# Half of K projected earlier, SyncE's list reordered, and the rows of maxima split straight from PSUM

## The reference, cut to what matters

```python
x = x + xattn(layernorm(x), ctx)
# inside: 16 heads of 16 channels
q = (query @ Wq + bq); k = (key_value @ Wk + bk); v = (key_value @ Wv + bv)
attn = einsum('bhqd,bhkd->bhqk', q, k) * scale
attn = clip(attn, -CLAMP, CLAMP)
attn = softmax(attn); attn = where(any(isnan(attn)), 1 / Nkv, attn)
x = einsum('bhqk,bhkd->bqhd', attn, v).reshape(B, Nq, C) @ Wo + bo
```

## Time and profile before

| What | Value |
|---|---|
| median of 3 runs | 1042.63 us (1041.19 to 1042.75) |
| profiled execution, its own time | 1051.74 us |
| its span | 1049.9 us |
| busy in the span: PE, PEld, DVE, ACT, POOL | 81%, 59%, 69%, 52%, 28% |
| mean granted clock of PE | 0.878 |

### The profile page before, as it was taken

One profiled execution on the slowest core, in us unless ns is written; L12 is line 12 of the kernel. 1 busy time (PEld: TensorE's weight loads), 2 busy tenths in 40 slices (PEclk: granted clock), 3 DMA queues, 4 the chain that ended last, 5 costly groups with the idle time before them and its releaser, 6 DMA issues.

```text
span 1049.9 us, 22128 instructions
## 1 busy us (share of the span) xinstructions
PE 845.6 (81%) x7942; PEld 619.5 (59%) x7942; DVE 720.2 (69%) x1464; ACT 551.0 (52%) x1211; POOL 297.5 (28%) x268
## 2 busy tenths in 40 slices
PE   3777777877788877779889999997546888878995
PEld 2355555555555555558756777774114776648995
DVE  7666666666666668876666766655698667676866
ACT  3344555455555433653355556536787556374542
POOL 2245433333343341504052111003633000063300
PEclk9987999898989876599999999996556889698997
DMA  6533445455455533742345566344210000100001
GB/s 170 108 104 93 113 108 120 111 115 115 125 133 138 116 110 117 238 138 67 96 115 157 160 193 196 109 126 137 62 37 8 1 1 0 58 22 2 3 2 64
DMA packets 81632, 102.02 MB, mean 97 GB/s; under 512 B 22935, under 2 KB 65714, under 8 KB 81483
## 3 DMA queue, kind: packets, MB, share of 16 engines
q1 hardware_dynamic: 72666, 92.31, 32.5%
q0 software_dynamic: 6144, 7.42, 2.7%
q10 hardware_dynamic: 2752, 1.39, 0.5%
HBM read 85.66 MB, written 15.19 MB: 96 GB/s over the span
## 4 chain that ended last, share of the span: by engine, by line
PE 43%; DVE 17%; DMA 14%; issue 9%; ACT 9%; SPq 3%; POOL 2%; ACTq 2%; DVEq 0%; POOLq 0%
PE ps L1185 10%; PE ps L1172 7%; DMA qs<-q_parts 3%; PE ps L1689 3%; DMA floor<-floor_q 3%; DMA inverse<-inv 3%; PE ps L2133 2%; PE ps L522 2%; PE ps L427 2%; PE ps L1683 2%; ACT area L1645 2%; POOL mTl L475 1%; PE ps L1636 1%; DMA k_parts<-kp 1%; PE ps L2144 1%
## 5 line engine op out<-in xcount | busy, mean ns | idle before, releaser
L509 DVE TENSOR_REDUCE m<-ps 100x2 f32<-100x722 f32 x128 | 115.6, 907 | 93.9 <-PE ps L504 92.5
L1234 ACT ACTIVATE hT<-ps,cols 128x500 f32<-128x500 f32 (+1 forms) x96 | 62.5, 651 | 107.0 <-PE ps L1172 88.4
L529 ACT ACTIVATE p<-ps 121x600 f32<-121x600 f32 x128 | 85.5, 668 | 59.3 <-PE ps L522 55.9
L544 DVE SCALAR_TENSOR_TENSOR p<-p,xe 121x600 f32<-121x600 f32 x128 | 105.5, 825 | 14.7 <-DMA xe<-floor 14.7
L1185 PE MATMUL ps<-w_h,hT_h 128*125 128x256 f16 (+1 forms) x384 | 105.4, 275 | 7.4 <-DVE x L1281 6.8
L1185 PE MATMUL ps<-w_l,hT_h 128*125 128x256 f16 (+1 forms) x384 | 105.3, 274 | 0.0
L1185 PE MATMUL ps<-w_h,hT_l 128*125 128x256 f16 (+1 forms) x384 | 105.3, 274 | 0.0
L1241 DVE TENSOR_TENSOR hT_l<-hT,hT_h 128x500 f16<-128x500 f32 (+1 forms) x96 | 62.3, 651 | 62.6 <-ACT hT_h L1235 57.9
L1077 POOL DMA_INDIRECT xe<-tokens,slot_of x32 | 45.6, 1424 | 153.0 <-PE ps L1195 100.8
L522 PE MATMUL ps<-qs,ks 128*121 128x100 f16 x768 | 72.6, 236 | 19.8 <-DMA qs<-mTl 11.0
L522 PEld LDWEIGHTS ps<-qs,ks 128*121 128x121 f16 x768 | 65.2, 152 | 36.4 <-ACT p L529 16.2
(11 more groups left out here) (341 smaller groups left out, 2193.5 us busy)
## 6 DMA issues: line engine op xcount, KB each, us to landing
xe<-floor SPq DMA_DIRECT2D x32, 378.1 KB
sw<-in_L_ffn_w_dram SPq DMA_DIRECT2D x16, 512.0 KB, 6.9
sw<-in_L_ffn_w_dram SPq DMA_DIRECT2D x8, 1024.0 KB, 5.7
stage<-in_L_xattn_W_f_dram SPq DMA_DIRECT2D x6, 1024.0 KB
k_parts<-kp SPq DMA_DIRECT2D x32, 181.5 KB, 3.7
ks<-k_parts SPq DMA_DIRECT2D x32, 181.5 KB
ctx_f<-in_ctxT_dram SPq DMA_DIRECT2D x16, 270.8 KB, 4.6
stage<-in_ctxT_dram SPq DMA_DIRECT2D x8, 541.5 KB
```

The costliest lines, as they stand in the source:

```text
L509: v.tensor_reduce(m32[p][:, 2 * i:2 * i + 2], ps[0:T, at:at + 2, 0:KV], AX.X, ALU.max).then_inc(m_max, 1)
L529: s.activation(p32[:, i % HALF, :, :, :].rearrange("p j n t -> p n j t"), ps[0:KT, t_bank(i):t_bank(i) + 2, 0:KJ * T].rearrange("p n (j t) ...
L544: v.scalar_tensor_tensor(probs, probs, 1.0, low, ALU.min, ALU.max).then_inc(a_cv, 1)
L1234: s.activation(hT[:, f % 3, 0:m], bank[2 + f % 2][:, 0:m], ACT.Silu, bias=bias, scale=1.0 / WS)
```

## The change: what it does

1. Half 0 of K is projected half a batch earlier: for batch b+3 at step 7 of batch b. Half 1 takes the place at step 1 that half 0 had, and q of b+3 takes the place at step 5 that half 1 had. ACT's and POOL's parts move with them.
2. The maxima are no longer copied to `mrow`. ACT casts the high part and takes the floor's exp straight from PSUM, ahead of the exp of the step. DVE, instead of POOL, makes the low part from PSUM (`m_low`). PSUM bank 7 is free after that, not after ACT's copy.
3. The floor's store is issued by SP. SP's list has a new order.

```diff
-        mT = [sba(f"mT{n}", [H // 2, 2, T], F16) for n in "hl"]
+        mT = sba("mT", [H // 2, 2, 2, T], F16)
-        mrow = sba("mrow", [H // 2, 2, T])
...
         def m_scalar(s, b, half):
             s.wait_ge(m_mm, 2 * b + half + 1)
-            wait(s, m_l, 2 * b + half - 1)
-            s.copy(mrow[:, half, :], UB_[0:NP, 0:T]).then_inc(m_t, 1)
-        def m_parts_scalar(s, b, half):
-            s.wait_ge(m_t, 2 * b + half + 1)
             wait(s, mr_in, 32 * (2 * b + half - 1))
-            s.copy(mT[0][:, half, :], mrow[:, half, :]).then_inc(m_h, 1)
+            s.copy(mT[:, half, 0, :], UB_[0:NP, 0:T]).then_inc(m_h, 1)
             wait(s, floor_dma, 32 * (2 * b + half - 1) - 16)
-            s.activation(floor_q[:, half, :], mrow[:, half, :], ACT.Exp, scale=-float(D) ** -0.5, bias=floor_bias[:, :]
+            s.activation(floor_q[:, half, :], UB_[0:NP, 0:T], ACT.Exp, scale=-float(D) ** -0.5, bias=floor_bias[:, :]
                          ).then_inc(l_e, 1)
-        def m_gpsimd(g, b, half):
-            g.wait_ge(m_h, 2 * b + half + 1)
-            wait(g, mr_in, 32 * (2 * b + half - 1))
-            g.tensor_tensor(mT[1][:, half, :], mrow[:, half, :], mT[0][:, half, :], ALU.subtract).then_inc(m_l, 1)
+        def m_low(v, b, half):
+            v.wait_ge(l_e, 2 * b + half + 1)
+            v.tensor_tensor(mT[:, half, 1, :], UB_[0:NP, 0:T], mT[:, half, 0, :], ALU.subtract).then_inc(m_l, 1)
         def rows_scalar(s, b, p, half):
-            s.wait_ge(m_h, 2 * b + half + 1)
             wait(s, mr_in, 32 * (2 * b + half))
             for n in range(2):
-                if n == 1:
-                    s.wait_ge(m_l, 2 * b + half + 1)
+                s.wait_ge((m_h, m_l)[n], 2 * b + half + 1)
...
-            floor_store(s, b, half)
 a_tensor:
-                if i == 1 and has(b, 2): k_tensor(pe, b + 2, p, 0, (m_t, 2 * b + 2))
+                if i == 1 and has(b, 2): k_tensor(pe, b + 2, p, 1, (m_l, 2 * b + 2))
-                if i == 5 and has(b, 2): k_tensor(pe, b + 2, p, 1, (m_t, 2 * b + 3))
+                if i == 5 and has(b, 3): q_tensor(pe, b + 3, q, (m_l, 2 * b + 3))
-                if i == 7 and has(b, 3): q_tensor(pe, b + 3, q, (y_x, b - 1) ...)
+                if i == 7 and has(b, 3): k_tensor(pe, b + 3, q, 0, (y_x, b - 1) ...)
 a_scalar:
-                i == 0: q_scalar(b + 2)      i == 2: k_scalar(b + 2, 0)    i == 6: k_scalar(b + 2, 1)
+                i == 0: k_scalar(b + 2, 0)   i == 2: k_scalar(b + 2, 1)    i == 6: q_scalar(b + 3)
 a_vector, ahead of s_vector and clip_vector of the step:
+                if i == 1: m_low(v, b, 1)
+                if i == 5 and has(b, 1): m_low(v, b + 1, 0)
 a_gpsimd:
-                i == 1: m_gpsimd, q_gpsimd(b + 2)   i == 3: k_gpsimd(b + 2, 0)   i == 5: m_gpsimd   i == 7: k_gpsimd(b + 2, 1)
+                i == 1: k_gpsimd(b + 2, 0)          i == 3: k_gpsimd(b + 2, 1)                      i == 7: q_gpsimd(b + 3)
 a_sync, the whole list (waits and the guards left out):
-            inv_load(b - 2); half_load(b + 1, 1); q_store(b + 2); floor_load(b, 1); den_load(b - 1);
-            k_store(b + 2, 0); half_load(b + 2, 0); context_load(b + 4); floor_load(b + 1, 0);
-            inv_store(b - 1); k_store(b + 2, 1)
+            q_store(b + 2); half_load(b + 1, 1); inv_load(b - 2); floor_store(b, 1); k_store(b + 2, 0);
+            den_load(b - 1); floor_load(b, 1); k_store(b + 2, 1); half_load(b + 2, 0); context_load(b + 4);
+            floor_store(b + 1, 0); inv_store(b - 1); floor_load(b + 1, 0)
 before the loop, ACT and PE:
-            m_parts_scalar(s, 0, 0); rows_scalar(s, 0, 0, 0)
+            rows_scalar(s, 0, 0, 0); floor_store(s, 0, 0); q_scalar(s, 2, 0)
-            q_tensor(pe, 2, 0, (m_t, 1))
+            q_tensor(pe, 2, 0, (m_l, 1)); k_tensor(pe, 2, 0, 0, (q_32, 3))
```

More of the change, by code:

```diff
@@ L278, in build @@
         s_mm, a_s, a_p, a_cv, a_pv = (sem(f"a_{n}") for n in ("s1", "s", "p", "clip", "pv"))
-        m_max, m_c, m_mm, m_t, m_h, m_l = (sem(f"m_{n}") for n in ("max", "c", "mm", "t", "h", "l"))
+        m_max, m_c, m_mm, m_h, m_l = (sem(f"m_{n}") for n in ("max", "c", "mm", "h", "l"))
         l_e, floor_dma, mr_in = (sem(n) for n in ("floor_e", "floor_dma", "m_rows_in"))
@@ L650, in a_tensor @@
                 if i == 0:
-                    m_tensor(pe, b, 1, (q_32, b + 3) if has(b, 2) else (yb_ev, 3) if has(b, 1) else (y_x, b - 2))
+                    m_tensor(pe, b, 1, (k_32, 2 * b + 5) if has(b, 2) else (yb_ev, 3) if has(b, 1) else (y_x, b - 2))
                 if i == 1 and has(b, 2):
-                    k_tensor(pe, b + 2, p, 0, (m_t, 2 * b + 2))
+                    k_tensor(pe, b + 2, p, 1, (m_l, 2 * b + 2))
                 if i in (2, 3) and has(b, 1):
                     v_tensor(pe, b + 1, q, i - 2, (v_ev, 2 * b + 3) if i == 3 else
-                             (k_32, 2 * b + 5) if has(b, 2) else (yb_ev, 4))
+                             (k_32, 2 * b + 6) if has(b, 2) else (yb_ev, 4))
                 if i == 4 and has(b, 1):
                     m_tensor(pe, b + 1, 0, (v_ev, 2 * b + 4))
-                if i == 5 and has(b, 2):
-                    k_tensor(pe, b + 2, p, 1, (m_t, 2 * b + 3))
+                if i == 5 and has(b, 3):
+                    q_tensor(pe, b + 3, q, (m_l, 2 * b + 3))
                 if i == 6 and from_(b, 2):
-                    y_tensor(pe, b - 2, (k_32, 2 * b + 6) if has(b, 2) else
-                             (m_t, 2 * b + 3) if has(b, 1) else (m_t, 2 * b + 2))
+                    y_tensor(pe, b - 2, (q_32, b + 4) if has(b, 3) else
+                             (m_l, 2 * b + 3) if has(b, 1) else (m_l, 2 * b + 2))
                 if i == 7 and has(b, 2) and not has(b, 3):
@@ L666, in a_tensor @@
                 if i == 1 and has(b, 1) and not has(b, 2):
[L667 removed]
+                    guard_even_tensor(pe, (m_l, 2 * b + 2))
                 if i == 7 and has(b, 3):
[L669 removed]
+                    k_tensor(pe, b + 3, q, 0, (y_x, b - 1) if from_(b, 2) else (q_32, b + 4))
         def a_scalar(s, b, t, p):
@@ L674, in a_scalar @@
                 if i == 0 and has(b, 2):
-                    q_scalar(s, b + 2, p)
+                    k_scalar(s, b + 2, p, 0)
                 if i == 1:
@@ L678, in a_scalar @@
                 if i == 2 and has(b, 2):
-                    k_scalar(s, b + 2, p, 0)
+                    k_scalar(s, b + 2, p, 1)
                 if i in (3, 4) and has(b, 1):
@@ L683, in a_scalar @@
                     m_scalar(s, b + 1, 0)
-                if i == 6 and has(b, 2):
-                    k_scalar(s, b + 2, p, 1)
+                if i == 6 and has(b, 3):
+                    q_scalar(s, b + 3, q)
                 exp_scalar(s, b, i)
                 if i == 1:
-                    m_parts_scalar(s, b, 1)
                     rows_scalar(s, b, p, 1)
                 if i == 5 and has(b, 1):
-                    m_parts_scalar(s, b + 1, 0)
                     rows_scalar(s, b + 1, q, 0)
@@ L698, in a_scalar @@
                     o_scalar(s, b - 1, q)
-                if i in (2, 6) and has(b, 2):
-                    k_high(s, b + 2, i // HALF)
+                if i in (0, 2) and has(b, 2):
+                    k_high(s, b + 2, i // 2)
                 if i in (4, 5) and has(b, 3):
@@ L710, in a_vector @@
                     m_vector(v, b + 1, q, 0)
+                if i == 1:
+                    m_low(v, b, 1)
+                if i == 5 and has(b, 1):
+                    m_low(v, b + 1, 0)
                 if i == 7 and from_(b, 2):
@@ L730, in a_gpsimd @@
             for i in range(NP):
[L731 to L734, removed]
+                if i == 1 and has(b, 2):
+                    k_gpsimd(g, b + 2, 0)
                 if i == 1 and not has(b, 1):
@@ L738, in a_gpsimd @@
                     if has(b, 2):
-                        k_gpsimd(g, b + 2, 0)
+                        k_gpsimd(g, b + 2, 1)
                     on_gpsimd(g, b - 2, p) if from_(b, 2) else x_bias_gpsimd(g, 2 * b)
@@ L747, in a_gpsimd @@
                     x_bias_gpsimd(g, 2 * b + 1)
-                if i == 5 and has(b, 1):
-                    m_gpsimd(g, b + 1, 0)
                 if i in (5, 6) and has(b, 3):
                     c_gpsimd(g, b + 3, q, i - 5)
-                if i == 7 and has(b, 2):
-                    k_gpsimd(g, b + 2, 1)
+                if i == 7 and has(b, 3):
+                    q_gpsimd(g, b + 3)
         def a_sync(sp, b, t, p):
             q = 1 - p
-            if b >= 2 and has(b, 1):
-                inv_load(sp, b - 2)
+            if has(b, 2):
+                q_store(sp, b + 2, t + 1, p)
             if has(b, 1):
@@ L762, in a_sync @@
                 half_load(sp, b + 1, q, 1)
+            if b >= 2 and has(b, 1):
+                inv_load(sp, b - 2)
+            floor_store(sp, b, 1)
             if has(b, 2):
-                q_store(sp, b + 2, t + 1, p)
-            floor_load(sp, b, 1)
+                k_store(sp, b + 2, t + 1, p, 0)
```

(19 more changed lines are left out.)

2 lines of the change are left out of this document (1 added, 1 removed).

## The result

The changed kernel took 1031.15 us (median of 5, 1029.85 to 1038.37) against 1042.63: ratio 0.9888, 95% interval 0.9853 to 0.9924. It is faster, by 11.5 us where 28.3 were forecast. A second measurement, on another chip, gave 0.9832 (0.9787 to 0.9878). The profiled execution took 1038.37, its span is 1036.3 (1049.9 before).

A forecast was written before the change was run, and what follows sets the result against it. PE was taken as nearest to the bound, SP's waits as a second bound. 2.25 us a batch over batches 1 to 13 is 29.3, plus 0.5, less 1.5: 28.3 off 1042.63, forecast 1014.3 us, range 1006 to 1022.

The forecast's parts named there:

- The rows: Maxima straight from PSUM: DVE's subtraction takes 0.22 us, no stall on DVE; charged -0.25 us a batch in all.
- ACT: ACT at step 1: k starts when PE has it; V's wait falls from 1.55 to 0.3 us a batch, +1.25.
- the walk of PE's list: PE's time per batch at full clock: 20.8 less 1.33, 0.85, 0.45 and 0.1, 18.1 us before charges.
- The step that failed: SP's new order: waits for K's stores go, most of the inverse's are hidden, loads issue earlier; +0.85 us a batch.
- the sum for SP's cycle: SP's new list per batch: loads, two floor's stores seen behind a load, q's store, floor's reads and K's store; 18.0 us.
- the 2.25 a batch: Gain per batch of the first attention: 1.25 + 0.3 + 0.1 + 0.85 - 0.25, from 21.43 to 19.2 us.
- A: Rival, chance 0.24: SP binds, its cycle of 18.0 lacking several items; period 20.2 us, 1027 us in all.
- C: Rival, chance 0.07: slower, floor's stores on SP's queue seen 8.0 us behind a load, deciding beyond 7.6; 1054 us.
- B: Rival, chance 0.10: all idle time goes and the clock holds; 3.4 us a batch, 1000 us in all.
- D: Rival, chance 0.04: no difference, rows land with the load as late as now and DVE's full charge is 1.2; 1042 us.
- Theory V: Theory stated with the experiments: the work moved to DVE costs the kernel time; its cost would show as above 1.000.
- The opening: Batch 0's first scores come 2.4 us later, the last K that falls away gives 0.94 back; -1.5 us.

The follow-up runs named there:

- y1_store_ahead: x1 with the floor's store of half 1 issued ahead of the read of the inverse, not behind it; ratio 0.9591 to the kernel before.
- y3_all_of_it: Changed kernel with the inverse's read in four, on its own semaphore, behind the floor's store; a semaphore per floor half; x loads on ACT; 995.92 us, 0.9511.
- x1: Changed kernel with a semaphore of its own for the read of the inverse, so the denominators' load no longer waits for it; ratio 0.9757 to the kernel before.
- x4: Changed kernel with two entries of SP's list exchanged: the floor's load of half 1 ahead of the denominators' load; ratio 0.9747 to the kernel before.
- z1: Changed kernel with only the floor's store of half 1 put ahead of the inverse's read, the denominators' wait left in; ratio 0.9851 to the kernel before.
- y2: Changed kernel with the four loads of x issued by ACT in batches 12 and 13, not by SP in 9 to 12; ratio 0.9756 to the kernel before.
- y0: The changed kernel, unaltered, measured again on another chip; ratio 0.9832 to the kernel before.
- z4: Changed kernel with the floor's two stores issued by ACT again, behind the rows; ratio 0.9862 to the kernel before.
- z3: Kernel before with only the rows of maxima taken straight from PSUM and the low part made on DVE; ratio 0.9913 to the kernel before.

## Why the prediction was wrong
**Right, step by step.** The rows: the subtraction takes 0.243 us (0.22 taken) and DVE never idles ahead of it, with PE's bank free in time. ACT: V's wait fell to 1.9 in eleven batches, where 0.3 a batch was said (3.3). SP's waits for K's stores went. And the walk of PE's list, 18.1 us a batch, was right to 0.6: with SP's loop opened, y1_store_ahead runs a batch in 17.47 and y3_all_of_it in 17.59.

**The step that failed** is SP's, in two sentences. "the inverse is stored ahead of the floor's load and read behind the next load, which hides most of 33.1": the wait for the inverse's store did go, but a wait for the read's own landing came, 58.5 us, nearly twice what was removed. It stands in `den_load` of the kernel before, as `wait(sp, den_dma, 48 * b)`, where the read had been issued 9.4 us ahead of the denominators' load (that entry followed the floor's wait), so it cost nothing and left no row. The change moved the two to within one small store and one K store of each other. "each stands behind work that is ready by then" was said of den's load without pricing this: the landing of the read, and the wait for it, were put at nothing.
So the sum for SP's cycle, 18.0, held the wrong terms: twice 6.3 for a floor's store seen, where the changed trace has 6.7 (read) + 0.6 (denominators) + 4.8 (the floor's load, for which the other half's store waits) + 4.5 (store seen) + 3.4 (issues, and the half load behind q's store) = 20.0. "The two meet, so neither is reached" took SP's cycle to be no longer than PE's walk, and it is longer by 2. x1, x4, y1 and z1 show the cause: taking the wait away gives 0.8 to 1.4%, putting the store ahead of the read 1.7% more, and the second without the first nothing.

**Where the time was missed.** Most of it is not in the undisturbed batches, where the 2.25 a batch came out as 2.02, 1.6 us short over the seven from batch 2 to 9. It is in the batches with a load of x, which the prediction did not name: the four from batch 9 to 13 were to gain 9.0 us and lost 8.2, 17.2 in all. From the output projection of batch 13 to the attention's last the kernel takes 59.4 us, after 54.4 before, 5.0 more. The failed step has a part in this: in those batches SP's loop passes a read that lands after 9.3 to 9.5 us, not 6.7 (the last of them, at 331.38, in batch 13), while the kernel before, whose loop did not pass it, had 21.4 there. It is not the whole: with the loop opened and the x loads left in place (y1) the four batches still take 20.3 each, the others 17.5. Moving the loads (y2) takes these four batches from 22.6 (y0) to 19.3 in the traces, and gives 0.8%, 8 us, in the times. That the undisturbed batches came out near the forecast is in part luck: a cycle of 20.0 that the sum had at 18.0 stood close to a period of 19.2 that was reached by adding PE's idle remainders.

**The rivals.** A was the closest: SP binds, period 20.2, 1027. Three of the four items that it says the cycle "lacks" are links of the measured loop (the inverse's read, the wait for den, the broadcast of the floor), and its sign came: DVE waits 3.5 us a batch for the floor. It was given 0.24; measured are 20.59 and 1031. C, the floor's store harmed by SP's queue, does not hold in the undisturbed batches, where a store on SP's queue is seen within 4.4 to 6.3 us and ACT's queue is no faster (z4); behind a load of x, though, such a store took 8.5 us (x1, issued at 248.74) and 8.6 (x4, at 247.64), beyond C's 7.6. B's state was reached only by further edits: y3_all_of_it holds the full clock and lies at 996. D fell with the result. Theory V falls with z3: the part alone makes the kernel faster, by 0.9%.

**The opening** was set to cost 1.5. Its first part came as said: batch 0's first scores start 6.1 us after ACT first takes the maxima (57.44 and 51.31), against 3.7 before (55.66 and 51.98), 2.4 more, though the load of exp's table, of which the sum had part of 0.7, takes 1.28 by itself in both traces. But the output projection of batch 2 is 7.5 us earlier than before, where the terms give about 2: batches 0 and 1, in which SP does not yet issue the read of the inverse, gained more than was said. No run separates this. Of the 13.6 us between the two profiled spans 8.4 are there at the end of the attention; the other 5.2 arise behind it, in code that is the same, and stay unexplained.

## What to carry to other kernels
When a list of DMAs is put in a new order, write down for each entry every semaphore that it waits on, those that are long satisfied too, and how far ahead of it the waited transfer is issued in the new order; a wait with no row in the trace can become the longest one. Count a loop in landings, not in issues: a store, read and store that wait for one another close a loop which no engine's busy time shows. A large transfer issued inside such a loop can cost what it did not cost before (here 23.4 us a batch after 21.4); look at the batches that hold one apart from the mean. And where a counted semaphore is shared by a small transfer and a large broadcast, whatever waits for the small ones waits for the large one too: a second semaphore and the small store ahead of the large read gave 2.4% here (0.9832 to 0.9591).

## What the runs showed of the hardware
- A transfer of a few KB is seen later behind a large one: the floor's 3 KB store is seen after 5.86 us behind a 200 KB read (x1), after 3.9 ahead of it (y1), and after 8.5 in a batch with a 400 KB load (x1). On another engine's queue it was no faster (4.5 to 4.9 us in z4, 4.4 to 4.6 in the changed kernel).
- A 128-partition read from a source with an outer size of 4 ran at a DMA share of 0.27 and landed after 6.7 us; as four reads of 32 partitions, 3.9 after the last issue and 5.4 after the first, for 1.3 us more of issuing.
- The granted clock was higher where PE idled less: 0.93 over 103 to 339 us in the changed kernel, 1.00 over 103 to 325 in y3_all_of_it. In y1_store_ahead it was 1.00 in the batch of 17.47 us and 0.86 in that of 22.18, where much the same matmuls (215 and 214 records) were busy for 15.60 and 18.20 us. The idle sum alone does not tell: the batch of 19.40 us idled 3.7 us at 1.00, that of 22.18 idled 4.0 at 0.86.
